# A two-bank rotation for the turned probabilities in the attention stages of a single-core Flamingo-style decoder

## What is computed

```python
qh = (x @ wq + bq)          # 112 queries, split over heads
kh = (memory @ wk + bk)     # 375 keys (112 in the self-attention of layer 2)
vh = (memory @ wv + bv)
a = softmax(qh @ kh.T / sqrt(d))     # masked in some layers
out = (a @ vh) @ wo
```

## Time and profile before

| | us |
|---|---|
| median of 3 runs | 1913.39 |
| lowest, highest | 1908.18, 1920.59 |
| the profiled execution's own time | 1915.56 |
| its span, first to last instruction | 1913.8 |
| PE busy | 1534.9 (80% of the span) |
| DVE busy | 803.4 (42%) |
| ACT busy | 674.3 (35%) |
| POOL busy | 215.3 (11%) |

### The profile page before, as it was taken

How to read it: one execution, slowest core, us unless ns; L and a number is a source line. 1 busy time by engine, 2 the same in 40 slices (tenths; PEclk the granted TensorE clock), 3 DMA queues, 4 the chain that set the end, 5 groups by cost and what they waited for, 6 DMA issues and landing times.

```text
span 1913.8 us, 34703 instructions
## 1 busy us (share of the span) xinstructions
PE 1534.9 (80%) x11511; PEld 1245.6 (65%) x11511; DVE 803.4 (42%) x2884; ACT 674.3 (35%) x2117; POOL 215.3 (11%) x326
## 2 busy tenths in 40 slices
PE   5977767879889889758469966487998999999954
PEld 4666655768776666536358955366896777787733
DVE  3545445441116565656301126563004443344456
ACT  2513413232106656426023325262333444244411
POOL 0000000000001111111221122014500000000000
PEclk9988988889999999867579988587999999999977
DMA  9300000128601100400169830112951001000000
GB/s 351 117 1 1 0 4 32 33 99 285 182 6 48 48 2 2 158 1 1 66 226 351 300 131 21 46 44 99 319 199 33 2 2 33 2 1 1 2 0 20
DMA packets 103092, 156.23 MB, mean 82 GB/s; under 512 B 12199, under 2 KB 80928, under 8 KB 102248
## 3 DMA queue, kind: packets, MB, share of 16 engines
q1 hardware_dynamic: 97355, 143.53, 22.7%
q0 software_dynamic: 3552, 9.18, 1.4%
q10 hardware_dynamic: 2048, 1.84, 0.3%
HBM read 147.31 MB, written 11.67 MB: 83 GB/s over the span
## 4 chain that ended last, share of the span: by engine, by line
PE 74%; DVE 8%; issue 6%; ACT 4%; DMA 4%; POOL 3%; SPq 1%; DVEq 1%; ACTq 0%; POOLq 0%
PE psum L491 51%; PE psum L560 8%; PE psum L584 6%; PE psum L544 5%; ACT arena L749 2%; DMA moe_b<-in_moe_b 2%; PE psum L479 2%; ACT arena L761 1%; SPq L889 1%; POOL rstd L461 1%; POOL stream L1111 1%; PE psum L592 1%; POOL token_rows L1083 1%; DMA region<-in_l_wv 1%; DVE x_state L823 1%
## 5 line engine op out<-in xcount | busy, mean ns | idle before, releaser
L491 PE MATMUL psum<-region,arena 128*125 128x128 f32 (+4 forms) x2160 | 372.7, 327 | 50.0 <-DVE arena L697 15.7
L491 PEld LDWEIGHTS psum<-region,arena 128*125 128x125 f32 (+2 forms) x2160 | 304.3, 191 | 113.5 <-issue 24.9
L749 ACT ACTIVATE arena<-arena,rowmin 112x375 f32<-112x375 f32 (+1 forms) x584 | 292.1, 505 | 187.4 <-DVE rowmin L668 187.1
L491 PE MATMUL psum<-arena,region 128*128 128x112 f32 (+2 forms) x1984 | 347.2, 335 | 4.2 <-DVE x_state L1738 1.7
L491 PEld LDWEIGHTS psum<-arena,region 128*128 128x128 f32 x1984 | 283.4, 205 | 69.3 <-issue 12.2
L560 PE MATMUL psum<-identity,arena 112*125 112x112 f32 (+1 forms) x1240 | 177.7, 287 | 30.9 <-ACT arena L761 14.8
L560 PEld LDWEIGHTS psum<-identity,arena 112*125 112x125 f32 (+1 forms) x1240 | 145.0, 180 | 87.1 <-ACT arena L761 26.6
L479 PE MATMUL psum<-identity,arena 112*128 112x112 f32 x176 | 39.0, 391 | 148.1 <-DVE arena L471 96.6
L491 PE MATMUL psum<-arena 128*128 128x128 f32 (+4 forms) x896 | 138.7, 313 | 0.5 <-DMA moe_b<-in_moe_b 0.5
L544 PE MATMUL psum<-arena 32*112 32x375 f32 (+3 forms) x912 | 134.8, 486 | 0.1
L491 PEld LDWEIGHTS psum<-arena 128*128 128x128 f32 (+2 forms) x896 | 124.7, 189 | 11.8 <-issue 0.9
(11 more groups left out here) (220 smaller groups left out, 1598.0 us busy)
## 6 DMA issues: line engine op xcount, KB each, us to landing
stream<-in_moe_w SPq DMA_DIRECT2D x36, 1024.0 KB, 7.4
arena<-in_moe_w SPq DMA_DIRECT2D x36, 1024.0 KB, 7.4
arena<-in_ctxT SPq DMA_DIRECT2D x32, 375.0 KB, 3.8
stream<-in_e_wg SPq DMA_DIRECT2D x8, 512.0 KB, 4.7
stream<-in_e_wu SPq DMA_DIRECT2D x8, 512.0 KB, 5.8
stream<-in_e_wd SPq DMA_DIRECT2D x8, 512.0 KB, 6.7
region<-in_e_wg SPq DMA_DIRECT2D x8, 512.0 KB, 7.6
region<-in_e_wu SPq DMA_DIRECT2D x8, 512.0 KB, 8.4
```

The lines of the kernel that those rows point to most:

```text
L491: last = pe.matmul(dst, l, r, start=(i == 0), stop=(i == n - 1))
L749: last = act.activation(e, e, ACT.Exp, bias=rowmin[:, j, n:n + 1], scale=-1.0, accum_out=rowsum[:, j, h:h + 1])
```

## The change

`turn_probs`, `keep_probs` and the signals take a `move`: one key tile of all four lanes. Key tile 0 goes to bank 4, key tile 1 to bank 5, key tile 2 again to bank 4, when ACT has copied key tile 0 out of it. ACT copies moves 0 and 2, DVE move 1. In stage 4 move 0 is lanes 0 and 1, move 1 lanes 2 and 3, and there is no move 2. `PT` becomes two sets of buffers by the parity of r, so the copies wait for `probs_used` of r-2. `turn_probs` waits once, for the `probs` of lane 3. Scores run two steps ahead of the turning, `outputs_of(r)` follows in the same step. The inverted sums go to bank 4, and the values of the four lanes to banks 4, 5, 5, 4; bank 6 is no longer used in attention. The functions are generators now, run to the end by `through`, which changes no instruction.

```diff
-        turned_inv, outs = bank[6], bank[7]
+        turned_inv, outs = bank[4], bank[7]
         def value_bank(j):
-            return bank[4 + j % 2]
+            return bank[(4, 5, 5, 4)[j]]
...
             def values_of(m, j):
-                if j >= 2:
-                    pe.wait_ge(*p["v_ready"].at(it, m, j - 2))
+                if j == 2:
+                    pe.wait_ge(*p["v_ready"].at(it, m, 1))
+                if j == 3 and m == 0:
+                    pe.wait_ge(*p["v_ready"].at(it, m, 0))
+                if j == 3 and m:
+                    pe.wait_ge(*p["rinv_T"].at(it, m - 1))
...
-            def turn_probs(r):
+            def turn_probs(r, move):
                 m, s = r // a.steps, r % a.steps
-                if s:
-                    pe.wait_ge(*p["probs_T"].at(it, r - 1))
+                if move == 2:
+                    pe.wait_ge(*p["probs_T"].at(it, r, 0))
+                elif s == 0:
+                    if move == 0:
+                        pe.wait_ge(*p["v_ready"].at(it, m, LANES - 1))
+                elif move == 0:
+                    pe.wait_ge(*p["probs_T"].at(it, r - 1, a.moves - 2))
+                else:
                     pe.wait_ge(*p["probs_rest_T"].at(it, r - 1))
-                else:
-                    pe.wait_ge(*p["v_ready"].at(it, m, LANES - 1))
-                    if m:
-                        pe.wait_ge(*p["rinv_T"].at(it, m - 1))
-                for j in range(LANES):
-                    pe.wait_ge(*p["probs"].at(it, r, j))
-                    for i in range(a.group * a.key_tiles):
-                        dst, n = (bank[4 + j // 2], j % 2 * 2 + i) if a.whole_pairs else (bank[4 + i], j)
+                if move == 0:
+                    pe.wait_ge(*p["probs"].at(it, r, LANES - 1))
+                dst, n = bank[4 + move % 2], 0
+                for j in range(2 * move, 2 * move + 2) if a.whole_pairs else range(LANES):
+                    for i in range(2) if a.whole_pairs else (move,):
...
PE, the loop over the steps:
-                    if s >= 2:
-                        outputs_of(r - 2)
-                    if s + 1 < a.steps:
-                        scores_of(r + 1)
-                        turn_probs(r)
-                        continue
...
+                    turn_probs(r, 0)
+                    turn_probs(r, 1)
+                    yield
+                    if a.moves == 3:
+                        turn_probs(r, 2)
+                    if s + 2 < a.steps:
+                        scores_of(r + 2)
+                        yield
+                        outputs_of(r)
+                        yield
+                    elif s + 2 == a.steps:
+                        if more:
+                            keys_queries(m + 1, 0)
+                            yield
+                            keys_queries(m + 1, 1)
+                        yield
+                        outputs_of(r)
+                        yield
...
DVE, mask_and_min and keep_rest:
-                    wait_first(v, *p["probs_turned"].at(it, r - 2))
+                    wait_first(v, *p["probs_turned"].at(it, r - 2, a.moves - 1))
...
-                if r:
-                    v.wait_ge(*p["probs_used"].at(it, r - 1))
+                if r >= 2:
+                    v.wait_ge(*p["probs_used"].at(it, r - 2))
...
ACT, the loop over the steps:
-                    exps(r, 0)
-                    exps(r, 1)
-                    if s:
-                        keep_probs(r - 1)
-                    elif m:
-                        keep_sums(m - 1)
-                    exps(r, 2)
-                    exps(r, 3)
...
+                    exps(r + 1, 0)
+                    keep_probs(r, 0)
+                    yield
+                    exps(r + 1, 1)
+                    if a.moves == 3:
+                        keep_probs(r, 2)
+                    yield
+                    exps(r + 1, 2)
+                    exps(r + 1, 3)
```

More of the change, by code:

```diff
@@ L83, in phase_signals @@
             continue
-        width = 1 if name in one or name in ONCE else lanes
+        n, width = n if isinstance(n, tuple) else (n, 1 if name in one or name in ONCE else lanes)
         if name not in known:
@@ L106, in __init__ @@
         self.steps = heads // self.group
+        self.moves = 2 if self.whole_pairs else key_tiles
         self.stay = 2 if self.paired and not self.whole_pairs else 1
@@ L596, in attend_tensor @@
                 keys_queries(0, j)
+                yield
             values_of(0, 0)
             scores_of(0)
-            for j in range(1, LANES):
-                values_of(0, j)
+            yield
+            values_of(0, 1)
+            yield
+            values_of(0, 2)
+            yield
+            values_of(0, 3)
+            if a.steps > 1:
+                scores_of(1)
+            yield
             for m in range(a.tiles):
+                more = m + 1 < a.tiles
                 for s in range(a.steps):
@@ new lines, in attend_tensor @@
+                for j in range(2 if a.steps > 1 else 0, LANES):
+                    keys_queries(m + 1, j)
+                    yield
+                outputs_of(r)
+                values_of(m + 1, 0)
+                yield
+                scores_of(r + 1)
+                values_of(m + 1, 1)
+                yield
+                turn_sums(m)
+                values_of(m + 1, 2)
+                yield
+                values_of(m + 1, 3)
+                if a.steps > 1:
+                    scores_of(r + 2)
@@ L694, in scale_heads @@
             def scale_heads(m):
+                if m == 0 and out_free is not None:
+                    v.wait_ge(*out_free)
                 v.wait_ge(*p["probs_used"].at(it, (m + 1) * a.steps - 1))
@@ L701, in attend_vector @@
                 keep_q(0, j)
+                yield
             keep_v(0, 0)
             mask_and_min(0)
-            for j in range(1, LANES):
-                keep_v(0, j)
+            yield
+            keep_v(0, 1)
+            yield
+            keep_v(0, 2)
+            yield
+            keep_v(0, 3)
+            if a.steps > 1:
+                mask_and_min(1)
+            yield
             for m in range(a.tiles):
+                more = m + 1 < a.tiles
                 for s in range(a.steps):
@@ new lines, in attend_vector @@
+                if not more:
+                    yield
+                    yield
+                    scale_heads(m)
+                    yield
+                    continue
+                for j in range(2 if a.steps > 1 else 0, LANES):
+                    keep_q(m + 1, j)
+                    yield
+                keep_v(m + 1, 0)
+                yield
+                mask_and_min(r + 1)
+                keep_v(m + 1, 1)
+                yield
+                scale_heads(m)
+                keep_v(m + 1, 2)
@@ L731, in attend_scalar @@
+                yield
+                keep_v(m + 1, 3)
+                if a.steps > 1:
+                    mask_and_min(r + 2)
+                yield
         def attend_scalar(act, a, p, it):
@@ L770, in attend_scalar @@
                 keep_k(0, j)
+                yield
+            for j in range(LANES):
+                yield
+            for j in range(LANES):
+                exps(0, j)
             for m in range(a.tiles):
[L772 removed]
+                more = m + 1 < a.tiles
+                for s in range(a.steps - 1):
                     r = m * a.steps + s
[L774 to L790 removed]
+                    exps(r + 1, 0)
+                    keep_probs(r, 0)
+                    yield
+                    exps(r + 1, 1)
+                    if a.moves == 3:
+                        keep_probs(r, 2)
+                    yield
+                    exps(r + 1, 2)
+                    exps(r + 1, 3)
+                    yield
+                    if more and s + 2 == a.steps:
+                        keep_k(m + 1, 0)
+                        keep_k(m + 1, 1)
+                        yield
+                r = (m + 1) * a.steps - 1
+                keep_probs(r, 0)
+                yield
+                if a.moves == 3:
+                    keep_probs(r, 2)
+                if not more:
+                    yield
+                    yield
+                    keep_sums(m)
+                    yield
+                    continue
+                for j in range(2 if a.steps > 1 else 0, LANES):
+                    keep_k(m + 1, j)
+                    yield
+                yield
+                yield
+                exps(r + 1, 0)
+                exps(r + 1, 1)
+                keep_sums(m)
+                yield
+                exps(r + 1, 2)
+                exps(r + 1, 3)
+                yield
         def attend_gpsimd(g, a, p, it):
```

176 lines of the change are left out of this document (84 added, 92 removed).

## The result

| | before | after |
|---|---|---|
| median on one chip, 6 runs each, us | 1912.9 | 1970.17 |
| lowest, highest | 1908.18, 1920.59 | 1967.76, 1977.68 |
| profiled execution, its span | 1915.56, 1913.8 | 1970.94, 1969.3 |

The changed kernel takes 1.0296 times as long, interval 1.0266 to 1.0325: 3% slower. In a second comparison, on another chip, the ratio was 1.0313 (1.0293 to 1.0332).

A forecast was written before the change was run, and what follows sets the result against it. PE bounds stage 5; PE-ACT exchange sets the step in stages 1, 3 and 4. Stages 5, 3, 1, 2, 4 add 22.6 + 9.3 + 7.5 + 2.0 + 10.0 = 51.4 to 1915.56: 1967.0, as median 1965 us, range 1934 to 1988.

The forecast's parts named there:

- Stage 5: Last attention, PE-bound: waits for reused banks are paid in full, 11.3 us a turn, 22.6 for both turns.
- Value wait: Stage 5, tile to tile: values of lane 2 wait for DVE's copy of lane 1, 0.52 us.
- even step: Stage 5: the third move waits 0.44 us for ACT's copy, which follows an exponential.
- odd step: Stage 5, ACT free: exchange of 1.26 us against 0.92 of issue, so the third move waits 0.34.
- Steps of stage 3: A new chain from last exponential through both ACT copies makes the steady step 3.73 us against 3.62, +0.11.
- Stage 3's start: Start of an attention: values of lane 2 wait for DVE's copy of lane 1, 1.34 us.
- fourth rival: Dearer handovers: waits on ACT register instructions cost 0.1 to 0.15 more each, 16 us, giving 1981; chance 0.20.
- first rival: Faster: without the `probs_used` wait, steps in stages 1 and 3 fall to ACT's 3.37, giving 1897; chance 0.05.
- second rival: Partly hidden: value waits stand, only half of the turn waits show, 19 us, giving 1932; chance 0.15.
- third rival: Clock: stage 5 falls to stage 4's granted 0.80, some 80 us on top, giving 2045; chance 0.03.
- Stage 4: Self-attentions, two moves and one ACT copy: 0.2 a step, start 0.6, tile change 0.7; 10.0 us over four runs.
- Stage 2: One step only: its start costs about 1.0 us a turn, 2.0 in all; turning and copying come out even.

The follow-up runs named there:

- e1: Changed kernel with key tile 2 turned into a third bank, bank 6, without waiting for a copy: 1932.5 us, ratio 1.0062 to the kernel before.
- e2: Changed kernel with the value banks (4, 5, 4, 5), their waits and the sums' bank 6 as before: 1952.56 us, ratio 1.0161 to the kernel before.
- e4: Changed kernel with ACT's two waits before a copy swapped, so the late one stands on the copy: 1968.77 us, ratio 1.0243 to the kernel before.
- e7: Changed kernel with third bank, value banks and waits as before, and ACT's two waits swapped: 1908.11 us, ratio 0.9952 to the kernel before.
- e5: Kernel before with only two sets of buffers for turned probabilities, copies waiting for outputs of two steps earlier: 1891.9 us, ratio 0.9869.
- e9: e7 with a wait for each of the four lanes' probabilities instead of the single one: 1885.41 us, ratio 0.9837 to the kernel before.
- e8: e5 with one wait for lane 3's probabilities instead of one per lane: 1937.99 us, ratio 1.011 to the kernel before.
- e10: Changed kernel with only the four lane-by-lane waits put back, two banks kept: 1940.43 us, ratio 1.0112 to the kernel before.

## Why the prediction was right, and where it was not

The forecast was 1965 us, 2.7% slower; 1970.17 came, 3.0% slower. The largest part, stage 5, was right by its mechanism. That the total came within 5 us is in part luck: stage 3 was missed by 7.4 us, and stages 2 and 4 took 3.4 and 1.8 back. By its steps:

- **Stage 5: right.** The forecast's own sum, 8 x 0.78 + 3.64 + 1.34, is 11.2 a turn and 22.4, not 11.3 and 22.6; 24.2 came. Value wait 0.52 forecast, 0.47 seen; even step 0.44 and 0.44; tile 22.7 and 22.90. The odd step was 0.34 and is 0.44. Its chain 0.64 + 0.04 + 0.53 + 0.05 was to be 1.26; it is 1.39, as the copy comes 0.80 behind the start of the turning (1525.54 to 1526.34) instead of 0.68. Twice, e1 and e2, taking the cause away took the time away.
- **Steps of stage 3: mechanism right, size off.** The term "Sum 3.73 against 3.62" measured 3.94, above the 3.7 to 3.8 that was to show it. Each piece of the chain of work was right to 0.01; what was short were the handovers: 0.14 from the last read to the PE instead of 0.05, 0.77 from the turning to the first copy instead of 0.68, 0.72 instead of 0.68 for the second. Over 24 steps the 0.21 makes 5.0 of the 7.4 us by which stage 3 was missed; the rest is in its starts and ends and was not traced further. Stage 3's start is one row: values of lane 2 waited 1.18 (forecast 1.34).

```profile
603.77 2.69 PEld L503 LDWEIGHTS psum<-region,arena 128*125 128x125 f32 x24 [1.18 <-DVE arena L713]
```

- **The fourth rival** (dearer handovers) was therefore half right in size: +8 us, not +16. That is 0.21 in 32 steps of stages 1 and 3 (6.7) and 0.10 in 16 odd steps of stage 5 (1.6). e4 and e7 show that the order of ACT's two waits makes 0.07 to 0.08 of one such handover; the rest, such as the 0.14 from the exponential's read to the PE, has no experiment.
- **The first rival** (faster) failed as a forecast but named a real gain: e5 is that gain alone, 24.5 us on its chip. It was priced with an ACT floor of 3.37, and the floor is 3.22, because the pair of copies holds ACT for 0.84 (641.00 to 641.84, where the next exponential starts), not for its 0.97. In the changed kernel it is hidden under longer chains: with these taken away, in e9, the step is 3.21 again.
- **The second rival** (partly hidden) would have kept half of the turn waits away; all three waits of a tile stand in every row above.
- **The third rival** (the clock) did not happen: 0.99 in stage 5 with three idles in a tile, 0.98 in stage 3 with one or more in each step. The rule that was cited with it, the Trainium skill's "TensorE: Matmul & The Clock Gate", section "A second HAM failure mode: psum-queue depth-cycling", did not show itself here: the rotation through two banks left the clock at its upper level, 2.4 GHz, nearly all of the time in these stages. The fall that the rival feared was seen in e8, which has three banks, behind an idle of 1.17 us.
- **Stage 4: near by luck.** +8.2 for 10.0 forecast, but made of parts that the forecast did not hold apart. Taking the single wait out (e10) is worth 15.6 to 17.3 there, and some 11 at nearly equal clocks, so the rest of the change gave some 3 to 9 back. And 6.3 of the 8.2 lie in the last two self-attentions, where the granted clock was 0.78 and 0.74 instead of 0.84 and 0.82; how much of that is the clock's stays open.
- **Stage 2: wrong sign, by the clock.** The value wait came (0.65). In the first turn, at a granted clock of 0.87 in both kernels, the stage grew from 25.6 to 26.7 us, the 1.0 of the forecast. The second turn got shorter, because its outputs ran faster:

```profile
380.61 2.89 PE L503 MATMUL psum<-region,arena 128*125 128x128 f32 x24 [0.65 <-DVE arena L713]
...
386.92 2.93 PE L613 MATMUL psum<-arena 125*128 125x112 f32 x24 [0.70 <-ACT arena L843]
```

The same 24 matmuls had their weight loads spread over 5.19 us before, at a granted clock of 0.82 over 357.59 to 384.00; the clock was 1.00 over 366.52 to 390.50 here. In the repetition of the changed kernel the stage took 49.5 us in both turns, in the experiments 47.1 to 51.4. That is a clock which differs from run to run, and no effect of the change that these runs can show.

## What to carry to other kernels

Before a PSUM bank is saved, compare the exchange (end of the producer, copy, back again) with the issue time of what stands between two uses of the bank: here 1.39 us against 0.95 in stage 5, where the PE is busy 180.17 of 188.15 us and pays the difference every time. Waits lane by lane let the PE start turning while ACT's last exponentials still run; merging them into one cost 1.8 points (e10) and 2.4 (e8, a lower clock included) here. A change that joins a gain (two buffer sets, -1.3 points) with a saving of resources should be timed in its parts: e5, the gain alone, beats both kernels with a small edit, and e9, which keeps the new order as well, is not clearly faster than e5.

## What the runs showed of the hardware

- The order of two waits on one ACT instruction is seen in the time: with the late one on the register instruction ahead of it, ACT started 0.77 behind the start of the turning, with the late one on the copy itself 0.69. The Trainium skill ("Perfetto Trace Analysis", section "Identifying Dependency Chains") says that an instruction waiting on several engines may get extra wait instructions in front of it. The order of the changed kernel shows such a pair on ACT, L837 ahead of L843; the cost is this case's.
- ACT's rows overlap in the trace: exponentials whose rows are 0.60 and 0.19 long start every 0.59 to 0.60, and a 0.53 copy is followed after 0.41 to 0.43 by the next instruction. The floor of an ACT-bound step is a sum of distances between starts, not of lengths.
- Short idles did not bring the clock down in the changed kernel: stage 3 had the PE busy 81.57 of 96 us, with idle time in each 3.94 us step, at a granted clock of 0.98. In e8 it fell from 1.00 to 0.50 behind an idle of 1.17 us (604.03), and stayed at 1.00 behind one of 1.16 in the same tile (612.86). These runs show no size of idle that decides it.
